# The mixture's rounds: the output product in PSUM banks of its own, cut in three and placed behind the normed rows' transposes; the cross attention's norm applied by ScalarE

## The reference

```python
x = x + _L0_attn_ref(_layernorm(x), ...)             # out @ Wo + bo closes it
x = x + _L0_xattn_ref(_layernorm(x), ctx_1024, ...)  # 8 heads; windows of 4 share 64 keys
x = x + _L0_ffn_ref(_layernorm(x), ...)              # 8 experts, 2 per token

def _layernorm(x, axis=-1, eps=1e-05):
    m = jnp.mean(x, axis=axis, keepdims=True)
    v = jnp.var(x, axis=axis, keepdims=True)
    return (x - m) / jnp.sqrt(v + eps)

# in _L0_ffn_ref
xc = x.astype(jnp.bfloat16)
rms = jnp.mean(xf * xf, axis=-1, keepdims=True)
normed = (xf * jax.lax.rsqrt(rms + EPS) * norm_weight).astype(jnp.bfloat16)
scores, idx = jax.lax.top_k(logits, K)
```

## Time and profile before

| | |
|---|---|
| median of 3 runs | 2045.48 us (2040.12 to 2047.65) |
| the profiled execution | 2038.56 us, its span 2036.8 us |
| PE, DVE, ACT, POOL busy | 1861.0, 1299.9, 975.3, 970.7 us |
| the rounds | TensorE's first product at 903.57, its last count at 1028.88 |
| `joined` of tiles 1 to 7 starts at | 912.53, 923.24, 936.53, 951.49, 969.13, 983.75, 998.37 |

### The profile page before, as it was taken

One profiled execution on the slowest core, in us unless ns is written; L12 is line 12 of the kernel. 1 busy time (PEld: TensorE's weight loads), 2 busy tenths in 40 slices (PEclk: granted clock), 3 DMA queues, 4 the chain that ended last, 5 costly groups with the idle time before them and its releaser, 6 DMA issues.

```text
span 2036.8 us, 52538 instructions
## 1 busy us (share of the span) xinstructions
PE 1861.0 (91%) x21476; PEld 1544.5 (76%) x21476; DVE 1299.9 (64%) x2932; ACT 975.3 (48%) x1984; POOL 970.7 (48%) x783
## 2 busy tenths in 40 slices
PE   7999999999999999987649579999999999988994
PEld 5677777777777777766437479999899999987883
DVE  6667676767676766647756665456556554556983
ACT  3666666666666666532235233334443343344551
POOL 2555555555555555545633743344234333435441
PEclk9999999999999999999879789999999999999997
DMA  6101020101230100225134520000221000220000
GB/s 243 55 19 47 19 78 19 51 19 71 102 130 20 50 9 12 73 101 164 45 120 130 157 93 13 18 18 13 80 80 28 19 19 18 69 84 22 12 17 16
DMA packets 74606, 119.85 MB, mean 59 GB/s; under 512 B 8392, under 2 KB 64464, under 8 KB 70992
## 3 DMA queue, kind: packets, MB, share of 16 engines
q1 hardware_dynamic: 69392, 105.31, 15.4%
q0 software_dynamic: 2560, 6.30, 1.1%
q10 hardware_dynamic: 2416, 4.88, 0.7%
HBM read 76.61 MB, written 39.85 MB: 57 GB/s over the span
## 4 chain that ended last, share of the span: by engine, by line
PE 37%; POOL 5%; DVE 4%; DMA 3%; issue 3%; ACT 2%; SPq 1%; POOLq 0%; DVEq 0%; ACTq 0%
PE psum L265 12%; PE psum L276 8%; PE psum L2036 3%; PE psum L2024 2%; PE psum L2534 2%; PE psum L2010 1%; POOL b_yg L1487 1%; PE psum L225 1%; PE psum L2568 1%; POOL xs L1477 1%; PE psum L246 1%; PE psum L1352 1%; PE psum L1369 1%; ACT e_pr L2673 1%; DMA b_x_in<-in_x 1%
## 5 line engine op out<-in xcount | busy, mean ns | idle before, releaser
L774 POOL TENSOR_TENSOR a_sm<-a_sm,a_rsum 128x1024 f32<-128x1024 f32 x256 | 480.1, 1895 | 355.6 <-DVE a_rsum L808 353.2
L796 DVE CUSTOM_DVE_ANT_0 a_sm<-psum,a_strip 128x1024 f32<-128x1024 f32 x256 | 312.0, 1219 | 145.3 <-PE psum L628 145.3
L709 ACT ACTIVATE a_sm<-a_sm,a_mn 128x1024 f32<-128x1024 f32 x256 | 293.9, 1148 | 28.2 <-DVE a_mn L796 27.1
L714 ACT ACTIVATE a_pT<-psum 128x512 f32<-128x512 f32 x256 | 151.6, 592 | 272.4 <-PE psum L641 272.4
L641 PE MATMUL psum<-ident,a_sm 128*128 128x128 f32 x2048 | 275.2, 277 | 5.7 <-POOL a_sm L774 4.6
L641 PEld LDWEIGHTS psum<-ident,a_sm 128*128 128x128 f32 x2048 | 223.8, 140 | 62.9 <-issue 46.0
L656 PE MATMUL psum<-a_pT,a_V 128*64 128x256 f32 x2048 | 249.0, 385 | 0.6 <-ACT a_o L720 0.6
L656 PEld LDWEIGHTS psum<-a_pT,a_V 128*64 128x64 f32 x2048 | 136.1, 136 | 77.3 <-issue 22.1
L803 DVE COPY a_pT<-psum 128x512 f32<-128x512 f32 x256 | 174.9, 683 | 12.6 <-PE psum L641 5.4
L2120 ACT ACTIVATE g_val<-psum 128x512 f32<-128x512 f32 x64 | 38.0, 597 | 215.8 <-PE psum L2036 215.6
L628 PE MATMUL psum<-a_KH,a_QH 64*128 64x512 f32 x512 | 114.3, 443 | 2.5 <-DVE a_mn L796 2.5
(11 more groups left out here) (396 smaller groups left out, 3764.9 us busy)
## 6 DMA issues: line engine op xcount, KB each, us to landing
a_strip<-table SPq DMA_DIRECT2D x16, 960.0 KB, 6.7
oT<-a_o SPq DMA_DIRECT2D x64, 128.0 KB, 1.9
xs<-b_zeros SPq DMA_DIRECT2D x8, 1024.0 KB, 4.1
b_oT_in<-oT SPq DMA_DIRECT2D x7, 1024.0 KB, 5.7
y<-b_yb SPq DMA_DIRECT2D x23, 256.0 KB, 2.2
b_xs<-xs SPq DMA_DIRECT2D x23, 128.0 KB, 2.2
a_raw<-in_a_wqkv SPq DMA_DIRECT2D x7, 384.0 KB, 3.4
s_x<-in_x_rev SPq DMA_DIRECT2D x4, 512.0 KB, 8.2
```

Source lines behind the costliest of these rows:

```text
L709: a.activation(sm[:, st % RING, :], sm[:, st % RING, :], ACT.Exp, scale=-1.0, bias=mn[:, at:at + 1], accum_out=rsum[:, at:at + 1]).then_in ...
L714: a.activation(probs(st, 0), psum[:, 4, :].rearrange("p (k q) -> p k q", k=4), ACT.Copy).then_inc(sig("pT_act"), 1)
L774: g.tensor_tensor(sm[:, st % RING, :], sm[:, st % RING, :], rsum[:, at:at + 1].broadcast_to([P, T]), ALU.mult).then_inc(sig("scaled"), 1)
L796: v.tensor_tensor_reduce(out=sm[:, st % RING, :], in0=scores_banks(hl).rearrange("p c n -> p (c n)"), in1=strip[:, pair % 2, hl, qt * P:qt ...
```

## The change

It makes these edits:

- The output product takes banks 0 and 1 in turn, all other units of the rounds the six others.
- It is cut in three: `ay_0` two products, `ay_1` six, `ay_2` eight. `ay_0` stands between `mT` and `mg`, `ay_1` behind `bs`, `ay_2` behind `mr`. Round 0 keeps all of tile 1's.
- `h` is written by ScalarE: `x1` times the reciprocal root plus an offset, which GpSimd computes as minus the mean times the reciprocal root, in two small instructions before and behind the reciprocal root's. On ScalarE it stands behind the copy `nT`.
- GpSimd does the reciprocal root for `xc` right behind `scatter`, and the bias added to `x1` last.
- ScalarE's conversion of the experts' second weights `w2` is done in halves, in rounds 4 and 6.

```diff
     def order(r):
         a, b, c = r, r - 1, r - 2
-        every = [("ay", a + 1), ("mT", c), ("mg", c), ("bT", a), ("bp", b), ("by", b), ("bs", a), ("mr", c), ("ay_rest", a + 1)]
-        if r == 0:
-            every = [("ay", 1), ("ay_rest", 1)]
+        every = [("mT", c), ("ay_0", a + 1), ("mg", c), ("bT", a), ("bp", b), ("by", b), ("bs", a), ("ay_1", a + 1),
+                 ("mr", c), ("ay_2", a + 1)]
...
-            if stage != "ay_rest":
-                turns.add(sig, [(stage, s)], range(8))
+            if stage == "ay_0":
+                turns.add(sig, [("ay", s)], range(2))
+            elif stage[:2] != "ay":
+                turns.add(sig, [(stage, s)], range(2, 8))
...
-        def attended(s, t):
+        def attended(s, part):
             bank = banks("ay", s)
-            for k in range(HP):
-                last = pe.matmul(bank[:, t * D:(t + 1) * D], (early["next"] if s == 1 else slots[s % 3])[0][:, k, t * P:(t + 1) * P], wo[:, k, :],
-                                 start=k == 0, stop=k == HP - 1)
-            return last
+            for i in range(*((0, 2), (2, HP), (HP, PT * HP))[part]):
+                t, k = i // HP, i % HP
+                last = pe.matmul(bank[:, t * D:(t + 1) * D], (early["next"] if s == 1 else slots[s % 3])[0][:, k, t * P:(t + 1) * P],
+                                 wo[:, k, :], start=k == 0, stop=k == HP - 1)
+            if part == 2:
+                last.then_inc(sig("ay_ps"), 1)
...
-            if r == 4:
+            if r in (4, 6):
                 a.wait_ge(have("w2b"), 16)
-                a.activation(w2[:, :, :, :], w2b[:, :, :, :], ACT.Copy).then_inc(sig("wide"), 1)
+                some = slice(0, E0 // 2) if r == 4 else slice(E0 // 2, E0)
+                a.activation(w2[:, some, :, :], w2b[:, some, :, :], ACT.Copy).then_inc(sig("wide"), 1)
...
+            if 0 < s < NP:
+                a.wait_ge(sig("bn_off"), 2 * s)
+                a.wait_ge(sig("bT_ps"), s)
+                for t in range(PT):
+                    a.activation(h[:, t, :], x1[s % 2][:, t, :], ACT.Identity, scale=bn[2][:, t:t + 1],
+                                 bias=offset[:, t:t + 1]).then_inc(sig("bn_h"), 1)
...
             if s < NP:
+                g.wait_ge(sig("bn_var"), PT * (s + 1))
+                g.wait_ge(sig("bn_h"), PT * s)
+                g.tensor_scalar(offset[:, :], bn[1][:, :, 0], -1.0, None, ALU.mult).then_inc(sig("bn_off"), 1)
                 norm_rstd(g, sig, "bn", s, bn, mhalf)
+                g.wait_ge(sig("bn_off"), 2 * s - 1)
+                g.wait_ge(sig("bn_rstd"), s + 1)
+                g.tensor_tensor(offset[:, :], offset[:, :], bn[2][:, :], ALU.mult).then_inc(sig("bn_off"), 1)
...
             if c >= 1:
                 scatter(c - 1)
+            if b < NP:
+                norm_rstd(g, sig, "mn", b, mn, mhalf)
             if s + 1 < NP:
                 first_sum(s + 1)
...
-                norm_rstd(g, sig, "mn", b, mn, mhalf)
...
-            if s < NP:
-                v.wait_ge(sig("bT_ps"), s)
-                norm_apply(v, sig, "bn", s, x1[s % 2], h, bn)
```

More of the change, by code:

```diff
@@ L1270, in attention @@
                 banks.take(pe, "ay", s)
-                attended(s, 0)
-            elif stage == "ay_rest":
-                attended(s, 1).then_inc(sig("ay_ps"), 1)
+            if stage[:2] == "ay":
+                attended(s, int(stage[3]))
             elif stage == "bT":
@@ L1526, in gpsimd @@
                 g.tensor_tensor(ss[:, :], ss[:, :], mhalf[:, 0:PT], ALU.pow).then_inc(sig("m_rms"), 1)
+            if s < NP:
+                g.wait_ge(sig("bn_h"), PT * (s + 1))
+                g.tensor_tensor(x1[s % 2][:, :, :], x1[s % 2][:, :, :], over_tiles(bo_b[:, :], PT), ALU.add).then_inc(sig("x1_bo"), 1)
         scatter(NP - 1)
```

13 lines of the change are left out of this document (5 added, 8 removed).

## The result

The changed kernel takes 2055.95 us (median of 6 runs, 2053.51 to 2062.7) against 2045.53 for the kernel before in the same comparison (6 runs, 2040.12 to 2047.65): a ratio of 1.0067, 95% interval 1.0047 to 1.0087. It is **slower by 0.67%**, 10.4 us where 2.8, no measurable change, were forecast.

The account below looks back on a forecast made before the run. A chain of waits closed by VectorE and GpSimd bounded the 14.62 us round; TensorE would close the new one: 4.75 + 3.60 + 2.77 + 3.70 + 0.13 = 14.95 us. Net +2.8 us gave a median of 2048.3 us, range 2040 to 2058.

Parts of the forecast that it names:

- the new loop: Rounds: TensorE, all sixteen products behind the normed rows' transposes, closes the loop and releases `joined`; 14.95 us a round.
- The second `joined`: Round 1: it comes 3 to 5 us late, at 927.7 against 923.24 in the sum.
- the half clock on the product: Round 1: a 3.9 us TensorE idle is followed by granted clock 0.50, losing 1.69 us.
- the second term: TensorE, from the transposes of `h` to the six products: 3.60 us, kept from the old profile.
- the tail behind them: Behind the rounds: round 7's mixture norm starts at 10.65 instead of 11.90, -1.25 us; the tail keeps its order.
- A: Rival: TensorE's clock dips every round after a 2.7 us idle, +0.73 in five rounds, 2052.4 us; chance 0.18.
- B: Rival: TensorE's half clock lasts until the six products, 2.45 us a round, 2061.8 us; chance 0.10.
- The sign that I named for A and B: TensorE, each round: products of 5 us and more would show the forecast wrong.
- The pair: ScalarE's two instructions that write `h`: 0.84 us together, bounds 0.75 to 0.94.
- the two offset operations: GpSimd, before and behind the power: 0.3 us each, between 0.2 and 0.8.
- The `xc` pair: VectorE's two mixture norm instructions take 1.60 us instead of 0.73 beside GpSimd's addition; VectorE still ready before TensorE.
- `w2`'s halves: ScalarE's copy in halves, in the rounds: no cost, nor a gain of its own.

Follow-up runs that it names:

- e3: The changed kernel with five unused products behind the last eight, in TensorE's long pause; 1.0024 of the kernel before.
- e6b: The changed kernel with unused products in all three TensorE pauses (5, 2 and 1); 1.0024 of the kernel before.
- e1: The changed kernel with TensorE's old order (eight products at the round's head, eight at its end), the rest kept; 0.9994 of the kernel before.
- e2: The kernel before with only banks 0 and 1 for the output product and the six others for the rest; ratio 0.9982.
- e7: The kernel before with only ScalarE's norm for `h` and GpSimd's two offset operations; ratio 1.0012.
- e4: The changed kernel with the norm for `h` back on VectorE, without the two offset operations; 1.0049 of the kernel before.
- e14: The changed kernel with VectorE's norm for `h` and unused products in the three pauses, none in the last rounds; 1.0011 of the kernel before.
- e10: e5 with two unused products ahead of the gate's and three ahead of the values product; 0.9967 of the kernel before.
- e5: The changed kernel with TensorE's old order and VectorE's norm for `h`; own banks, GpSimd's order and `w2` halves kept; 0.9964 of the kernel before.
- e11: The kernel before with only GpSimd's new order (mixture's reciprocal root ahead of the next sum, x1's addition last); ratio 1.0007.

## Why the prediction was wrong

**What bounds the kernel, and the new loop: right.** From round 2 on `joined` is released by TensorE (idle 1.72), the normed rows' transposes start 2.56 us after it (2.6 forecast), all rounds are alike. The second `joined` is 3.3 us later than before (3 to 5 forecast); round 1 took 14.89, against 15.17 in the prediction's terms. There the forecast had the half clock on the product, for 1.69 us; it lay on the transposes of `h`, the values product and the scores, for 1.5 (916.28 to 920.19 is 3.91, against 2.40).

**The terms of the round:**

| term | predicted | round 6 | 
|---|---|---|
| `joined` to `h`'s transposes | 4.75 | 4.89 |
| from them to the six products | 3.60 | **5.60** |
| six products and the ranks | 2.77 | 2.72 |
| eight products, and until `joined` | 3.83 | 3.79 |
| sum | 14.95 | 17.00 |

The step that failed is the second term: "From them to the product's second half are 3.60 us (992.89-989.29); I keep that." It kept the full clock for pieces whose clock was in doubt. Measured are 5.60 us, since the clock was at 1.2 GHz from the transposes of `h` to the scores. Rounds 2 to 6 took 85.2 us, 10.5 more than five of 14.95.

The sum was made against the profiled execution, where it gives 2041.4; measured are 2053.51, 12.1 over. Of these, 10.5 are the rounds, 2.3 the tail behind them (below), -1.2 the start and round 1, and 0.5 lie behind the rounds. Against the median the miss is only 7.7, and 2055.95 lies inside the stated 2040 to 2058. That is luck: I added 6.9 us to get from the profiled execution to the median, and in the changed kernel that distance is 2.4.

**Where the doubt was weighed wrongly.** Rivals A and B named this place. A said that the clock dips and costs 0.73; B, that it stays down until the six products and costs 2.45 a round. Measured are 2.0 to 2.3, on average 2.1: it is B, whose clock came back during the scores. I gave it 0.10, on a comparison of one number, the pause: 2.60 us had kept the clock, 2.94 had lost it. But behind the pause of 2.60 stood 3.69 us of unbroken product, and behind the new one of 2.65 stand 0.40, 1.26 and 0.30 us and then a further wait. I had written that down in B ("as broken"), and gave it too little weight. The sign that I named for A and B, products of 5 us and more, never came: the half clock lay on the short pieces alone. e3 shows that the long pause matters, e6b that the short waits do too, e1 and e2 (round 6) that the clock can fall with no pause over 1.1 us ahead of it in the round. Pauses do not even order by length: in e7 one of 2.36 us was followed by half clock, in the kernel before one of 2.60 by full clock. The case in the rows nearest to it was not the pause of 2.94 but the last rounds of the kernel before, where the same short pieces ran at half clock.

The Trainium skill, "TensorE: Matmul & The Clock Gate", A second HAM failure mode: psum-queue depth-cycling, said of another kernel that small pauses between groups of products let the clock swing. By that rule B was the likelier, and here the trace agrees with it: 0.50 and 1.00 by turns in each round.

**The norm on ScalarE.** The pair took 1.09 us, not 0.84, outside the bounds of 0.75 to 0.94; the two offset operations took 0.41 and 0.19 for my 0.3 each. Together `h`'s transposes are 0.14 late, a small term. For the small operations the prediction says "No row shows them without a power"; the trace of the kernel before had one, the operation ahead of the power in the same round (L193, 128x2): 0.41 us. The row that I took as a price for the pair was nearest in size, but had one per-row operand, where this one has two (scale and bias). The Trainium skill, "ScalarE: Activation LUTs", What ACT_TABLE_LOAD costs, prices each per-row operand at about 93 ns, on top of 186 ns and 0.833 ns a column, by which one such instruction would be an estimate of 0.585 us. The list of this tile's instructions (shortest, median, longest in ns) agrees with 0.592 in the median:

```profile
L1440 ACT ACTIVATE b_h<-b_x1b,b_offset,b_bn_rs x8: 584/592/601, 915.1 to 1016.0; 128x256 f32<-128x256 f32 x8
```

The runs price the whole part, a round: nothing at half clock (e4 against the change), 0.2 in the new order with the clock held (e6b against e14), 0.3 to 0.4 in the old one (one round each: e1's 13.74 against 13.48 in e10 and 13.37 in e5), 0.6 to 0.8 in the kernel before (e7). It helped in none of them. The same page, Rules for kernel authors, gives additions and multiplications to VectorE, and these runs agree.

**GpSimd's order.** The `xc` pair took 1.61 us beside GpSimd's sum (1.60 forecast), and VectorE was ready before TensorE. What I missed is at the end: x1's addition now stands last in a round, and in round 7 VectorE's normed rows run into it. VectorE's row, then GpSimd's:

```profile
1026.25 1.87 DVE L1622 SCALAR_TENSOR_TENSOR b_nr<-b_xc,b_ss,b_nw 128x256 bf16<-128x256 bf16 x2 [0.19 <-POOL b_ss L1539]
```

```profile
1026.19 1.26 POOL L1542 TENSOR_TENSOR b_x1b<-b_x1b,b_bo_b 128x512 f32<-128x512 f32 x1
```

The pair took 0.88 before. So the tail from the seventh `joined` to the experts became 43.1 us, 1.0 longer, where I had it 1.25 shorter: the mixture's norm starts 12.1 us after `joined` as before (11.9), since `h` comes later and TensorE is at half clock there. That the 1.0 belongs to GpSimd's order is shown by e11, which has nothing else of the change: its tail is 43.1 too, with the pair at 1.87 (1014.87), while e2 and e7, which lack it, have 42.1 and 42.2.

**Hidden parts.** `w2`'s halves cost nothing, as said, and round 4 is no longer special; but e2 had 14.80 there with the whole copy, and e11 14.60 with the shared banks as well, so the 17.64 of before was not the copy's doing. One gain I had in hand and did not see: by my own sum GpSimd's order lets VectorE be ready at 13.65 (e5 shows 13.4 to 13.5), which with TensorE's old order would have been the length of the round.

**The account of the round**, in runs: 14.62 before; 13.5 with own banks and GpSimd's order; 14.7 with all products behind the transposes (e14; 14.3 as an estimate without its filling's delay); 14.86 with ScalarE's norm; 17.0 with the clock as it then falls. The change contains a gain of 1.1 us a round and spends it twice.

**Open.** Why the clock falls in one round and not in the next of the same kernel (e3, e5, e11) isn't settled; I found nothing in the timelines that tells the two apart. No run moved x1's addition alone in e5, which might give back the 1.0 us of the tail. How the 0.8 to 1.2 and 0.2 to 0.6 divide exactly is blurred by the filling.

## What to carry to other kernels

Price a stretch of short TensorE pieces at both clock levels before you put it on the path that closes a loop: as long as another engine closes the round a half clock is free, and the order that makes TensorE the closer turns the same dip into 2 us. When you look for a precedent in the trace, compare not only the length of the pause but what stands behind it. And test the parts of a change in pairs: own banks and GpSimd's order shortened a round at full clock by at most 0.2 us alone, and by 1.1 together.
